# Six-stage decoder: the high half of the probabilities straight behind the exponential

## The reference

```
x = ln(x + self attention 0(x))            16 heads of 128, causal, rotary
x = ln(x + cross attention 0(x, ctx))      1024 keys, RMS norm of q and k
x = ln(x + gated ffn, 4 experts(x))
x = ln(x + self attention 1(x))            16 heads of 128, causal
x = ln(x + cross attention 1(x, ctx))      1024 keys, 8 key heads for 16 query heads, masked
x = ln(x + ffn with fp8 rounding(x))
attention:  softmax(q @ k.T * scale) @ v, then @ Wo
```

## Time and profile before

| | |
|---|---|
| median of 3 executions | 2929.32 us (2920.0 to 3839.74) |
| the profiled execution: time, span | 2923.55 us, 2921.7 us |
| TensorE busy | 2509.2 us, 86% |
| VectorE busy | 1862.7 us, 64% |
| ScalarE busy | 1572.5 us, 54% |
| GpSimd busy | 864.7 us, 30% |
| ScalarE's idle time ahead of `ph`, and of that until `ri` | 461.6 us, 394.9 us |
| mean granted TensorE clock | 0.945 of 2.4 GHz |

### The profile page before, as it was taken

One profiled execution on the slowest core, in us unless ns is written; L12 is line 12 of the kernel. 1 busy time (PEld: TensorE's weight loads), 2 busy tenths in 40 slices (PEclk: granted clock), 3 DMA queues, 4 the chain that ended last, 5 costly groups with the idle time before them and its releaser, 6 DMA issues. The chain is left out here.

```text
span 2921.7 us, 60581 instructions
## 1 busy us (share of the span) xinstructions
PE 2509.2 (86%) x21768; PEld 1612.3 (55%) x21768; DVE 1862.7 (64%) x3317; ACT 1572.5 (54%) x2742; POOL 864.7 (30%) x741
## 2 busy tenths in 40 slices
PE   6888888888888898888978999989999999986454
PEld 4555555455655565566455666655566666643222
DVE  4666663366665666666155666651688888858886
ACT  4666663176766666666043555550577777732321
POOL 4556555400110010012232212223100000146675
PEclk9999998999999999999988999999999999998777
DMA  3333333144444444446230333341477777852000
GB/s 96 71 71 92 68 73 81 47 89 92 97 95 91 95 91 96 93 94 124 80 151 21 85 88 87 88 94 46 84 146 145 143 151 145 153 115 77 20 0 29
DMA packets 752867, 263.39 MB, mean 90 GB/s; under 512 B 724816, under 2 KB 724816, under 8 KB 751184
## 3 DMA queue, kind: packets, MB, share of 16 engines
q1 hardware_dynamic: 750960, 255.48, 41.0%
q0 software_dynamic: 1760, 5.77, 0.7%
HBM read 82.84 MB, written 2.10 MB: 29 GB/s over the span
## 5 line engine op out<-in xcount | busy, mean ns | idle before, releaser
L786 ACT ACTIVATE ph<-p,ri 128x1024 bf16<-128x1024 f32 (+4 forms) x512 | 437.4, 854 | 461.6 <-DVE ri L1056 394.9
L1066 DVE SCALAR_TENSOR_TENSOR pl<-p,ri,ph 128x1024 bf16<-128x1024 f32 (+4 forms) x512 | 517.4, 1010 | 129.6 <-issue 83.5
L1122 PE MATMUL ps<-wo_hi,v_hi 128*128 128x128 bf16 x2688 | 487.2, 222 | 79.4 <-DMA wo_lo<-pl 79.3
L1123 PE MATMUL ps<-wo_lo,v_hi 128*128 128x128 bf16 x2688 | 487.0, 222 | 0.0
L1124 PE MATMUL ps<-wo_hi,v_lo 128*128 128x128 bf16 x2688 | 486.9, 222 | 0.0
L797 ACT ACTIVATE p<-p,nb 128x1024 f32<-128x1024 f32 (+4 forms) x512 | 435.7, 851 | 48.4 <-DVE nb L1049 33.9
L1122 PEld LDWEIGHTS ps<-wo_hi,v_hi 128*128 128x128 bf16 x2688 | 266.7, 99 | 142.9 <-DMA wo_lo<-pl 96.0
L1122 PE MATMUL ps<-k_hi,q_hi 128*128 128x512 bf16 (+3 forms) x768 | 277.2, 361 | 45.9 <-issue 30.1
L1123 PEld LDWEIGHTS ps<-wo_lo,v_hi 128*128 128x128 bf16 x2688 | 266.9, 99 | 39.1 <-issue 0.8
L1124 PE MATMUL ps<-k_hi,q_lo 128*128 128x512 bf16 (+3 forms) x768 | 277.1, 361 | 0.0
L1123 PE MATMUL ps<-k_lo,q_hi 128*128 128x512 bf16 (+3 forms) x768 | 276.9, 361 | 0.0
(11 more groups left out here) (197 smaller groups left out, 6066.4 us busy)
## 6 DMA issues: line engine op xcount, KB each, us to landing
raw_kv<-in_wkvself SPq DMA_DIRECT2D x32, 512.0 KB, 3.9
raw_q<-in_wqself SPq DMA_DIRECT2D x32, 256.0 KB, 2.7
wo_hi<-ph SPq DMA_TRANSPOSE x512, 3.1
wo_lo<-pl SPq DMA_TRANSPOSE x512, 3.1
raw_q<-in_woself SPq DMA_DIRECT2D x32, 256.0 KB, 2.8
raw_q<-in_wqcross SPq DMA_DIRECT2D x32, 256.0 KB, 2.7
raw_q<-in_wocross SPq DMA_DIRECT2D x32, 256.0 KB, 3.0
raw_kv<-in_wkvcross SPq DMA_DIRECT2D x24, 256.0 KB, 3.1
```

The costliest lines, as they stand in the source:

```text
L786: nc.scalar.activation(m["ph"][:, qt % 2, 0:w], m["p"][:, qt % 2, 0:w], ACT.Copy, scale=ri[:, qt % 2:qt % 2 + 1]).then_inc(p_norm, 1)
L1066: nc.vector.scalar_tensor_tensor(out=m["pl"][:, qt % 2, 0:w], in0=m["p"][:, qt % 2, 0:w], scalar=ri[:, qt % 2:qt % 2 + 1], in1=m["ph"][:, ...
L1122: nc.tensor.matmul(o, l(0), r(0), start=first, stop=False)
L1123: nc.tensor.matmul(o, l(0), r(1), start=False, stop=False)
```

## The change

Three things change in the attention stages, and no arithmetic. The high half `rounded` of a tile moves from the start of the next tile to the place right behind the tile's own exponential, ahead of the jobs; `inverse`, which it needs, moves on VectorE from ahead of the next score pass to behind the `remainder` of the tile before. The transfers of high and low halves count two semaphores, `tr_hi` and `tr_lo`; ScalarE waits for the first, VectorE for the second, TensorE for both. And `heads_out` of ScalarE and VectorE comes behind `job_parts`.

```diff
-        tr_in = [sem(f"tr_in{i}") for i in range(QT)]
+        tr_hi, tr_lo = [sem(f"tr_hi{i}") for i in range(QT)], [sem(f"tr_lo{i}") for i in range(QT)]
...
-                    sp.dma_start_transpose(m["pT"][0][:, qt, 0:w // P, :], m["ph"][:, qt % 2, 0:w]).then_inc(tr_in[qt], 16)
+                    sp.dma_start_transpose(m["pT"][0][:, qt, 0:w // P, :], m["ph"][:, qt % 2, 0:w]).then_inc(tr_hi[qt], 16)
...
-                    sp.dma_start_transpose(m["pT"][1][:, qt, 0:w // P, :], m["pl"][:, qt % 2, 0:w]).then_inc(tr_in[qt], 16)
+                    sp.dma_start_transpose(m["pT"][1][:, qt, 0:w // P, :], m["pl"][:, qt % 2, 0:w]).then_inc(tr_lo[qt], 16)
...
ScalarE, rounded(n, it, qt)
-                        act.wait_ge(tr_in[bq], at(lambda n: 32 * (c["u"] + behind(n, qt, 2)[0] + 1), n, it))
+                        act.wait_ge(tr_hi[bq], at(lambda n: 16 * (c["u"] + behind(n, qt, 2)[0] + 1), n, it))
ScalarE, unit(n, it)
-                        if n or qt:
-                            rounded(*((n, it, qt - 1) if qt else (n - 1, it, QT - 1)))
                         act.wait_ge(s_max, at(lambda n: CREDIT + c["s"] + QT * n + qt + 1, n, it))
...
+                        rounded(n, it, qt)
+                        job_parts(n, it, qt, L.jobs(n, qt))
                         if qt == QT - 1 and n:
                             heads_out(n - 1, it)
-                        job_parts(n, it, qt, L.jobs(n, qt))
VectorE, remainder(n, it, qt)
-                        dve.wait_ge(tr_in[bq], at(lambda n: 32 * (c["u"] + behind(n, qt, 2)[0] + 1), n, it))
+                        dve.wait_ge(tr_lo[bq], at(lambda n: 16 * (c["u"] + behind(n, qt, 2)[0] + 1), n, it))
VectorE, unit(n, it)
-                        if n or qt:
-                            inverse(*prior)
                         scores(n, it, qt)
                         if n or qt:
                             remainder(*prior)
+                        inverse(n, it, qt)
+                        job_parts(n, it, qt, L.jobs(n, qt))
                         if qt == QT - 1 and n:
                             heads_out(n - 1, it)
-                        job_parts(n, it, qt, L.jobs(n, qt))
TensorE, weigh(n, it, qt)
-                    pe.wait_ge(tr_in[qt], at(lambda n: 32 * (c["u"] + n + 1), n, it))
+                    pe.wait_ge(tr_hi[qt], at(lambda n: 16 * (c["u"] + n + 1), n, it))
+                    pe.wait_ge(tr_lo[qt], at(lambda n: 16 * (c["u"] + n + 1), n, it))
```

More of the change, by code:

```diff
@@ L816, in _ @@
                 units(act, unit)
-                rounded(UNITS - 1, None, QT - 1)
                 heads_out(UNITS - 1, None)
@@ L1096, in _ @@
                 units(dve, unit)
-                inverse(UNITS - 1, None, QT - 1)
                 remainder(UNITS - 1, None, QT - 1)
```

## The result

The changed kernel takes **3113.62 us** (median of 4 runs, 3112.46 to 3122.15), the kernel before 2927.48 beside it: ratio 1.065, 95% interval [1.0625, 1.0676], so slower by 6.5%. One of the four runs of the kernel before took 3839.74 us, and the ratio leaves it out. The forecast was 3167 with a range from 3060 to 3235. The profiled execution has a span of 3111.6 us against 2921.7.

The account below looks back on a forecast made before the run. It took TensorE to bound cross1 and nearly self1, VectorE and ScalarE waiting for each other to pace self0, and cross0 to wait on `nq`; 101 + 77 + 51 + 14 = 243 us on 2923.55 gave 3167 us, range 3060 to 3235.

Parts of the forecast that it names:

- the main term: Attention tiles: rounding behind their exponential delays the next score pass, 1.4 us per 1024-column tile with anything behind its exponential.
- cross1, +101: Stage cross1: six tiles per two units pay 1.4 us each, 130 us, less 29 us of VectorE's slack: 101 us slower.
- self0, +77: Stage self0: the longer chain costs 2.5 us per unit, 31 units, all of it counting: 77 us slower.
- cross0, +51: cross0: tiles shift 1.4, 1.4, 0.1, -1.1 us per unit, 56 us, less 5 at the loop's turn: 51 slower.
- self1, +14: Stage self1: the middle between 50 us if nothing absorbs the shift and 23 us of idle time regained: 14 us slower.
- One landing semaphore per half ... Both cost nothing: Attention tiles: TensorE's two more waits per tile are satisfied with the old one; no cost, gain only where ScalarE waits.
- Its waits for landings should be nearly gone: Sign: TensorE's waits for transposed low halves to land, 79.3 us over the whole run before, should nearly vanish.
- the clock falls: Rival: in self0 query and key matmuls after the long pause run at 1.2 GHz, 78 us more, 3245 us; chance 0.10.
- the short form: TensorE in self0, after its longest pause: slow matmuls fall into time in which it would wait anyway.
- The bound stays TensorE: Rival: VectorE and ScalarE have room for longer chain; 79 us of landing and 34 of `nq` waits return; 2811 us, chance 0.05.
- only the two first stages pay: Rival: in cross1 TensorE sets the pace as before; only 77 + 51 + 14 and a few us, 3070 us; chance 0.12.
- It moves little: Rival: rounding ends up beside VectorE's remainder, hops of 0.47 us repaid by landings; 2900 to 2980 us, chance 0.06.

## Why the prediction was right, and where its sizes were off

Direction, mechanism and range held. The chain of the main term is there instruction by instruction, and putting the high half back took 291 us off. Of the four terms two were near (86 for 101, 99 for 77), and two were far too high (5.9 for 51, 0.6 for 14). By its steps:

- *cross1, +101.* Measured +86. The distances with one projection are 5.06 where the text had 5.1, those without 2.77. Not every tile paid 1.4: the eight places pay 1.37, 1.38, 0.79, 1.00, -0.01, -0.04, -0.02 and 1.33, together 5.80 per pair, 15.5 times 90 us, where the text had 8.4 per pair, 130, less 29 of slack. The projection tiles with the longest distances before (4.27, 5.31, 5.08) paid least. In the pair of units at 2322 us of the kernel before, the tile of 5.08 holds a wait for scores of 1.30 us and that of 4.27 one of 0.46; the 29 us count these. They leave 11 to 15 us, of which the tile of 5.31, where the heads' output changed its place, has about 6. With one semaphore cross1 grows by 93. The share of TensorE is 88%, not 83.
- *self0, +77.* Measured +99. The even units took 16.1 and 15.8 us, 2.5 to 2.8 more than before, as forecast (2.5). The odd ones took 18.2, 4.4 more; 1.9 too many in about 14 units is 27 us, the excess and a little more. The missed term is VectorE's stretch beside GpSimd's weight split. In the kernel before it is there too, mostly on the remainder of 384 columns (1.54 us in odd units, 0.62 in even ones) and little on `k_lo` (1.02 and 0.69), but an odd unit is only 0.45 longer than an even one. In the changed kernel both are stretched (1.60 and 2.32 us), and the third distance of odd units, 5.06 for 2.85, holds most of the excess. The sum counted hops and durations from quiet tiles and never asked what lay beside them.
- *cross0, +51.* Measured +5.9. The mechanism was right: 1.37, 1.38, 0.02 and -1.13 by the medians against 1.4, 1.4, 0.1 and -1.1. `nq` starts 2.93 us after the score pass, where the text had 2.9. What was mis-sized is the loop's turn, to which I gave 5 us. With the old semaphore cross0 is longer by 40.5 us, not far from the forecast; the other 34.6 came back with the extra instruction in TensorE's program, and not through slack in tile 0.
- *self1, +14.* Measured +0.6. The text took the middle between two ends and had no row for it. The shift went into waits that ScalarE had in this stage: those for job matmuls fell from 34.0 to 0.5 us, and those for a landing ahead of `ph` from 51.5 to 21.7. With the old semaphore the stage is longer by 8.6.
- *"One landing semaphore per half ... Both cost nothing"* is the step that failed. The text gave this part nothing; it brought 46 us to the kernel before and 54 to the changed one, 34.6 of them in cross0. The thing that I called free, a wait already satisfied, was not free of consequences as an instruction. The text's own exception, a gain where ScalarE waits for that landing, may be the other 19 us; the text put it at nothing, holding that on the new chain the landing is long past. The changed kernel without that part measured 3167.47 us. That it meets the forecast's 3167 is luck: self0's excess (+26) is cancelled by cross0 (-11), cross1 (-8) and self1 (-5).
- *"Its waits for landings should be nearly gone"* was wrong. They fell from 43.5 to 17.3 us in self0, stayed at 28 in self1 and rose from 5.6 to 12.7 in cross1. I read this as the low half landing late because it is made after the high one, whatever semaphore counts it; no run tests it.
- *`nq` near 1.1 us*: 1.28 (39.7 us, 31 times), right.
- *The rival "the clock falls".* The clock in self0 did fall, from 0.96 to 0.91, after pauses of up to 5.7 us. It cost next to nothing there, as the short form said: in the whole stage VectorE waits 2.4 us for scores and ScalarE 2.2 us for job matmuls. Its price shows in the kernel with the heads' output left in front, where the slow matmuls lie on the path in cross0. So what keeps the changed kernel clear of it is the third part of the change.
- *"The bound stays TensorE"* and *"only the two first stages pay"*: excluded by cross1's 86 us and by TensorE's 47.7 us of waits for `q_lo`. *"It moves little"*: excluded by 6.5%.

## What to carry to other kernels

In a loop where two engines hand a tile back and forth, put what the other engine waits for first, and keep work that nobody wants at once for the time in which its engine waits anyway; between the two places of the same rounding lie 291 us here. Cost every added instruction by its place in the program too: if pauses that wait for nobody stand at a loop's turn, look whether the instruction queue moves packets inside the loop, and try an empty instruction before believing a mechanism. Before a long chain is moved, look at what the engines that share memory with it do in *each* kind of unit, and not only in a quiet one.

## What was unexpected of the hardware

- A TensorE program longer by one empty instruction per tile ran 41 us faster (2883 against 2924); code fetches fell from 114 to 61, and 24.7 us of "issue" pauses of TensorE in cross0 went, with the half-clock matmuls that followed them. The slower programs moved nine packets of 16 KB on the instruction queue in every turn of cross0's loop, the faster ones, all longer by one instruction per tile in the four stages, none.
- A VectorE instruction of 0.69 us took 2.38 beside a GpSimd subtraction of 2.12 us.
- With waits of 3.7 us for `nq` (115.2 us, 31 times) in place of 1.3, cross0's last distance rose from 7.56 to 12.74 us, 5.2 for a wait longer by 2.4; behind the one shown TensorE stood at a clock of 0.50, and from `nq` to the next score pass it took 7.24 us in place of 4.63. Here the longer wait cost about twice its length.
